# Layer norm moments moved from VectorE to GpSimd in a fused state-space and mixture-of-experts kernel

## The reference, cut to what matters

```python
def _layernorm(x, axis=-1, eps=1e-05):
    m = jnp.mean(x, axis=axis, keepdims=True)
    v = jnp.var(x, axis=axis, keepdims=True)
    return (x - m) / jnp.sqrt(v + eps)

# attn: y = causal convolution of (x B^T) with a Cayley-eigenvalue kernel, times C^T, + D * x
# ffn: 8 experts, h = silu(x Wg) * (x Wu), out = sum over experts of (h Wd) * cw, cw from two softmaxes
x = L0_attn_u
x = x + _layernorm(_L0_attn_ref(_layernorm(x), ...))
x = x + _layernorm(_L0_ffn_ref(_layernorm(x), ...))
```

## Time and profile before

| | us |
|---|---|
| median of 3 runs | 1160.89 (1160.76 to 1161.62) |
| the profiled execution | 1161.8 |
| its span in the trace | 1160.0 |
| PE busy | 1135.0 (98%) |
| DVE busy | 922.2 (80%) |
| ACT busy | 698.0 (60%) |
| POOL busy | 639.0 (55%) |

### The profile page before, as it was taken

The page is one execution under the profiler, slowest core; times in us unless marked ns, Lnnn a source line. Parts: engine busy times, 40 slices in busy tenths (PEclk is TensorE's granted clock), DMA queues, the critical chain, the costliest instruction groups (busy, mean ns, idle before and its releaser), DMA issues.

```text
span 1160.0 us, 16822 instructions
## 1 busy us (share of the span) xinstructions
PE 1135.0 (98%) x5110; PEld 933.6 (80%) x5110; DVE 922.2 (80%) x1999; ACT 698.0 (60%) x1358; POOL 639.0 (55%) x492
## 2 busy tenths in 40 slices
PE   7799999999999999999999999999999999999996
PEld 5577888888888888888888888888888888888885
DVE  7788887888778788887888778788887888778665
ACT  3576565655656556565655656566565665756563
POOL 2686564555646555464645546455464655556453
PEclk8899999999999999999999999999999999999999
DMA  3330212102121020211102021110212102020110
GB/s 96 103 108 19 74 37 55 38 20 77 34 64 47 32 52 28 74 38 56 36 20 83 28 65 46 44 39 28 74 37 65 41 9 81 28 73 28 46 56 10
DMA packets 82697, 57.61 MB, mean 50 GB/s; under 512 B 35344, under 2 KB 64176, under 8 KB 82608
## 3 DMA queue, kind: packets, MB, share of 16 engines
q1 hardware_dynamic: 82608, 56.54, 16.5%
HBM read 48.13 MB, written 8.39 MB: 49 GB/s over the span
## 4 chain that ended last, share of the span: by engine, by line
PE 94%; DVE 3%; issue 1%; POOL 1%; ACT 0%; DMA 0%; SPq 0%; POOLq 0%; ACTq 0%; DVEq 0%
PE g L270 10%; PE u L270 10%; PE y L270 10%; PE g L272 10%; PE g L271 10%; PE y L272 10%; PE u L272 10%; PE u L271 10%; PE y L271 10%; PE n_ps L277 2%; PE m_ps L270 1%; PE m_ps L271 1%; PE m_ps L272 1%; PE m_ps L353 1%; PE m_ps L352 0%
## 5 line engine op out<-in xcount | busy, mean ns | idle before, releaser
L1061 POOL TENSOR_TENSOR hid_lo<-hid,hid_hi 128x512 fp32r<-128x512 f32 x255 | 341.1, 1338 | 409.1 <-ACT hid_hi L541 409.0
L535 ACT ACTIVATE gate<-g 128x512 f32<-128x512 f32 x512 | 305.7, 597 | 326.5 <-PE g L272 324.9
L797 DVE TENSOR_TENSOR hid<-gate,u 128x512 f32<-128x512 f32 x512 | 348.8, 684 | 164.1 <-ACT gate L535 132.7
L541 ACT ACTIVATE hid_hi<-hid 128x512 fp32r<-128x512 f32 x512 | 320.9, 627 | 37.7 <-DVE hid L797 37.1
L803 DVE TENSOR_TENSOR hid_lo<-hid,hid_hi 128x512 fp32r<-128x512 f32 x257 | 211.4, 823 | 1.8
L270 PE MATMUL g<-xe_hi,w_hi 128*128 128x512 f32 x512 | 206.7, 404 | 1.0 <-ACT gate L535 0.9
L270 PE MATMUL u<-xe_hi,w_hi 128*128 128x512 f32 x512 | 200.3, 391 | 4.1 <-DVE hid L797 4.1
L270 PE MATMUL y<-hid_hi,w_hi 128*128 128x512 f32 x512 | 200.4, 391 | 0.4 <-ACT hid_hi L541 0.2
L272 PE MATMUL y<-hid_hi,w_lo 128*128 128x512 f32 x512 | 200.1, 391 | 0.0
L271 PE MATMUL g<-xe_lo,w_hi 128*128 128x512 f32 x512 | 199.9, 390 | 0.0
L272 PE MATMUL g<-xe_hi,w_lo 128*128 128x512 f32 x512 | 199.9, 390 | 0.0
(11 more groups left out here) (173 smaller groups left out, 1141.3 us busy)
## 6 DMA issues: line engine op xcount, KB each, us to landing
cw_b<-cw_scratch SPq DMA_DIRECT2D x128, 256.0 KB, 3.4
x_sb<-x_in SPq DMA_DIRECT2D x16, 256.0 KB, 3.0
x_out<-o_sb SPq DMA_DIRECT2D x16, 256.0 KB, 2.2
out_scratch<-acc_t SPq DMA_DIRECT2D x60, 64.0 KB, 2.2
ffn<-out_scratch SPq DMA_DIRECT2D x15, 256.0 KB, 2.6
stage<-wgate_in SPq DMA_DIRECT2D x8, 256.0 KB, 2.7
stage<-wup_in SPq DMA_DIRECT2D x8, 256.0 KB, 3.0
stage<-wdown_in SPq DMA_DIRECT2D x8, 256.0 KB, 3.9
```

What stands on the lines that cost most here:

```text
L535: nc.scalar.activation(gate[:, k % 2, :], g_ps[k % 2][:], ACT.Silu).then_inc(gate_ready, 1)
L541: nc.scalar.activation(hid_hi[:, k % RING, :], hid[:, k % RING, :], ACT.Copy).then_inc(hi_ready, 1)
L797: nc.vector.tensor_tensor(hid[:, k % RING, :], gate[:, k % 2, :], u_ps[k % 2][:], ALU.mult).then_inc(hid_ready, 1)
L1061: nc.gpsimd.tensor_tensor(hid_lo[:, k % RING, :], hid[:, k % RING, :], hid_hi[:, k % RING, :].bitcast(f32), ALU.subtract).then_inc(lo_pool, 1)
```

## The change

POOL takes the five operations of mean and variance, and the shift, for the norms of x, y and x1 of chunks 1 to 15, and for the output norm of chunks 0 to 14. The two fused operations of DVE that it replaces become plain ones, so mean and variance take six operations on POOL (`moments`): an addition and a subtraction, two multiplications, a multiply-add by constants, and an addition. There are four semaphore steps of its own between them. The mean is kept with its sign turned (`minus_mean`), so that the shift is one multiplication and the norm of x adds it.

DVE keeps `bn_stats`, and the four tiles of the norm of x, which it now does after unit 4 and not unit 3. PE transposes them after unit 6 and not unit 5. The first chunk's mixer and the last chunk's output norm stay as they were, with functions of their own. The diff, cut to its core:

```diff
-TENSOR_AT = {"turn_cw": 4, "turn_x": 5, "bu": 9, "c": 15, "turn_y": 16, "turn_xe": 26,
+TENSOR_AT = {"turn_cw": 4, "turn_x": 6, "bu": 9, "c": 15, "turn_y": 16, "turn_xe": 26,
              "logits": 27}
-VECTOR_AT = {"weights": 1, "stats_x": 1, "var_x": 2, "norm_x": 3, "lo_x": 7, "enter": 8, "scan": 9,
-             "fin_turn": 6, "fin_stats": 14, "fin_var": 14, "fin_shift": 15, "leave": 12, "lo_w": 13, "y": 15, "stats_y": 16, "var_y": 16,
-             "shift": 18, "stats_x1": 22, "var_x1": 22, "shift_x1": 23, "lo_xe": 26, "softmax": 27, "exps": 30,
+VECTOR_AT = {"weights": 1, "stats_x": 1, "norm_x": 4, "lo_x": 7, "enter": 8, "scan": 9,
+             "fin_turn": 6, "fin_stats": 14, "leave": 12, "lo_w": 13, "y": 15, "stats_y": 16,
+             "stats_x1": 22, "lo_xe": 26, "softmax": 27, "exps": 30,
              "products": 31}
-GPSIMD_AT = {"rstd_x": 2, "fin_rstd": 15, "fin_add": 21, "rstd_y": 16, "residual": 18, "rstd_x1": 22}
+GPSIMD_AT = {"norm_x": 2, "fin_norm": 15, "fin_add": 21, "norm_y": 16, "residual": 18, "norm_x1": 22}
...
+            def moments(st, m, ve, link, at):
+                nc.gpsimd.tensor_tensor(m[:], st[:, :, 1:3], st[:, :, 4:6], ALU.add)
+                nc.gpsimd.tensor_tensor(ve[:], st[:, :, 1], st[:, :, 4], ALU.subtract).then_inc(link, 1)
+                pool.wait_ge(link, at + 1)
+                nc.gpsimd.tensor_tensor(m[:], m[:], minus_mean[:], ALU.mult)
+                nc.gpsimd.tensor_tensor(ve[:], ve[:], ve[:], ALU.mult).then_inc(link, 1)
+                pool.wait_ge(link, at + 2)
+                nc.gpsimd.tensor_scalar(ve[:], ve[:], 0.25, LN_EPS, ALU.mult, ALU.add).then_inc(link, 1)
+                pool.wait_ge(link, at + 3)
+                nc.gpsimd.tensor_tensor(ve[:], ve[:], m[:, :, 1], ALU.add).then_inc(link, 1)
+                pool.wait_ge(link, at + 4)
+
+            def mix_norm(c, n):
+                pool.wait_ge(stat_ready, 3 * (c - 1) + n)
+                moments(stats, mv, var_eps, norm_link, 12 * (c - 1) + 4 * (n - 1))
+                nc.gpsimd.tensor_tensor(rstd[:], var_eps[:], half[:], ALU.pow).then_inc(rstd_ready, 1)
+                if n > 1:
+                    pool.wait_ge(rstd_ready, 3 * c + n)
+                    nc.gpsimd.tensor_tensor(shift[:], mv[:, :, 0], rstd[:],
+                                            ALU.mult).then_inc(shift_ready if n == 2 else x1_shift_ready, 1)
...
+            def fin_norms(c):
+                pool.wait_ge(fin_stat, c + 1)
+                moments(stats2, mv2, var_eps2, fin_norm, 4 * c)
+                nc.gpsimd.tensor_tensor(rstd2[:], var_eps2[:], half[:], ALU.pow).then_inc(fin_rstd, 1)
+                pool.wait_ge(fin_rstd, c + 1)
+                nc.gpsimd.tensor_tensor(shift2[:], mv2[:, :, 0], rstd2[:], ALU.mult).then_inc(fin_shift, 1)
```

More of the change, by code:

```diff
@@ L138, in build @@
         cw_t = sb("cw_t", [E * NT, P])
+        minus_mean = sb("minus_mean", [P, NT, 2])
         stats2, mv2 = sb("stats2", [P, NT, 6]), sb("mv2", [P, NT, 2])
@@ L645, in normalise @@
                     last = nc.vector.tensor_scalar(dst[:, j, :], src(j), mv[:, j, 0:1], rstd[:, j:j + 1],
-                                                   ALU.subtract, ALU.mult)
+                                                   ALU.add, ALU.mult)
                 return last
@@ L654, in mix_stats_x, with early_var, scan_link @@
                 dve.wait_ge(x_loaded, 16 * (c + 1))
[L655 to L659, removed]
+                measure(lambda j: x_sb[:, j, :], stats, mix_link if c == 0 else stat_ready)
+            def early_var(n):
+                mean_var(stats, mv, var_eps, mix_link, (0, 5, 8)[n - 1]).then_inc(var_ready, 1)
+            def scan_link(c, n):
+                return 3 + n if c == 0 else 11 + 2 * (c - 1) + n
             def early_shift_x():
@@ L695, in mix_stats_y, with early_shift_y @@
                 dve.wait_ge(y_turned, c + 1)
-                measure(lambda j: n_ps[:, j * P:(j + 1) * P], stats, mix_link)
-            def mix_shift(c):
-                dve.wait_ge(rstd_ready, 3 * c + 2)
+                measure(lambda j: n_ps[:, j * P:(j + 1) * P], stats, stat_ready)
+            def early_shift_y():
+                dve.wait_ge(rstd_ready, 2)
                 shifts(shift, mv, rstd).then_inc(shift_ready, 1)
@@ L703, in mix_stats_x1, with early_shift_x1 @@
                 dve.wait_ge(x1_ready, c + 1)
-                measure(lambda j: x1[:, c % X1S, j, :], stats, mix_link)
-            def mix_shift_x1(c):
-                dve.wait_ge(rstd_ready, 3 * c + 3)
+                measure(lambda j: x1[:, c % X1S, j, :], stats, stat_ready)
+            def early_shift_x1():
+                dve.wait_ge(rstd_ready, 3)
                 shifts(shift, mv, rstd).then_inc(x1_shift_ready, 1)
@@ L779, in fin_stats_last, with fin_mean_var_last, fin_shifts_last @@
                 measure(lambda j: n_ps[:, j * P:(j + 1) * P], stats2, fin_link)
[L781 to L785, removed]
+            def fin_mean_var_last():
+                mean_var(stats2, mv2, var_eps2, fin_link, 0).then_inc(fin_var, 1)
+            def fin_shifts_last():
+                dve.wait_ge(fin_rstd, NCHUNK)
                 shifts(shift2, mv2, rstd2).then_inc(fin_shift, 1)
@@ L827, in _ @@
             nc.vector.memset(pair_mean[:, :, 1], 1.0 / D)
+            nc.vector.memset(minus_mean[:, :, 0], -0.5)
+            nc.vector.memset(minus_mean[:, :, 1], 1.0 / D)
             nc.vector.memset(sharp[:, :, 0, :], 1.0)
@@ L914, in _ @@
             nc.vector.bn_stats(stats[:, 3, :], u_ps[1][:, P:2 * P]).then_inc(mix_link, 1)
-            mix_var(0, 2)
-            mix_shift(0)
+            early_var(2)
+            early_shift_y()
             for j in range(NT + 1):
@@ L932, in _ @@
             last.then_inc(mix_link, 1)
-            mix_var(0, 3)
-            mix_shift_x1(0)
+            early_var(3)
+            early_shift_x1()
             for j in range(NT // 2):
@@ L1021, in _ @@
             fin_stats_last(NCHUNK - 1)
-            fin_mean_var(NCHUNK - 1)
-            fin_shifts(NCHUNK - 1)
+            fin_mean_var_last()
+            fin_shifts_last()
             for j in range(NT):
@@ L1073, in _ @@
                                     pattern=[[-1, P]], channel_multiplier=1).then_inc(const_ready, 2)
-            mix_rstd(0, 1)
+            early_rstd(1)
             pool.wait_ge(trig_ready, 1)
@@ L1081, in _ @@
                                     ALU.subtract).then_inc(proj_split, 1)
-            mix_rstd(0, 2)
-            mix_rstd(0, 3)
+            early_rstd(2)
+            early_rstd(3)
             pool.wait_ge(xn_ready, 2)
@@ L1101, in body @@
                     if not last:
[L1102 to L1105, removed]
+                        if k == GPSIMD_AT["norm_x"]:
+                            mix_norm(c + 1, 1)
+                        if k == GPSIMD_AT["norm_y"]:
+                            mix_norm(c + 1, 2)
                         if k == GPSIMD_AT["residual"]:
                             mix_residual(c + 1, 1 - par)
-                        if k == GPSIMD_AT["rstd_x1"]:
-                            mix_rstd(c + 1, 3)
+                        if k == GPSIMD_AT["norm_x1"]:
+                            mix_norm(c + 1, 3)
                     if not first:
-                        if k == GPSIMD_AT["fin_rstd"]:
-                            fin_rsqrt(c - 1)
+                        if k == GPSIMD_AT["fin_norm"]:
+                            fin_norms(c - 1)
                         if k == GPSIMD_AT["fin_add"]:
@@ L1117, in _ @@
             add_part(NCHUNK - 1, (NCHUNK - 1) % 2, E - 2)
-            fin_rsqrt(NCHUNK - 1)
+            fin_rsqrt_last()
 def sine_rows():
```

32 lines of the change are left out of this document (9 added, 23 removed).

## The result

The changed kernel takes 1180.9 us (median of 4 runs, 1179.85 to 1181.27), the kernel before 1161.26 beside it. The ratio is 1.0168, with a 95% interval from 1.0150 to 1.0185: slower, by some 19.6 us (1.7%). The profiled execution of the changed kernel has 1179.85 us, with a span of 1178.0, against 1161.8 and 1160.0 before.

What follows compares the result with a forecast made beforehand. PE, busy without a gap in the later chunks, was taken to bound the kernel. 15 chunks x (0.60 for x + 0.45 for x1) = 15.8 us on 1160.9 gave 1176.7, say 1177; range 1160.5 to 1203.

Steps and rivals of the forecast that it cites:

- PE has no gap in the later chunks: In the 14 later chunks PE is busy for all 969.40 us, so time DVE gets back is worth nothing there.
- Stall at the transposes of x: After unit 4 DVE's tiles lie beside two POOL operations and reach PE late: 0.6 us a chunk.
- A small operation on POOL takes 0.16 us: In POOL's norm chains, read off a line through 512 and 256 columns; bounds 0.10 and 0.40 us.
- X: Time from POOL being free to the shift of a norm: 2.48 us plus 0.5 for the port, 3.0 us.
- Y's shift comes earlier: At the norm of y, the shift is there at 501.0, so ACT gets 0.35 us earlier on and nothing stalls.
- Stall at the transposes of x1: POOL's chain starts after `hid_lo` of unit 21, so the shift comes 0.27 to 0.62 late, say 0.45 us a chunk.
- Chunk 0: nothing: In chunk 0 the small DVE operations free some tenths and the chain on POOL takes them back: nothing.
- What would show it: In 14 chunks PE idle 14 to 16 us, two waits for `xn` 14 or 15 times each, 70.3 us a chunk.
- the signs against: Small POOL operation over 0.25 us, PE waits for POOL's `hid_lo`, four tiles in 1.1 us, or a 69.2 us chunk.
- only one is late: Rival: only the norm of x late, 1170, or only the shift of x1, 1168; chance 0.20.
- Neither is late: Rival: tiles of x and shift of x1 both in time, 1161, or 1158 if chunk 0's idle goes; 0.15, faster 0.05.
- POOL is much slower with small operations: Rival: the ratio of 1.9 at 512 columns holds for small operations too, 1200, or 1223 at 0.40; chance 0.20.

Runs made afterwards that it cites:

- d: The changed kernel with the norm of x back in its old place and the output's residual sum moved from after unit 21 to after unit 24: 1163.53 us.
- e: The kernel before, all moments on VectorE, with only the norm of x one unit later: 1169.71 us against 1160.66.
- a: The changed kernel with the norm of x back in its old place (tiles after unit 3, transposes after unit 5), moments still on POOL: 1171.05 us.
- b: The changed kernel with DVE's four tiles of the norm of x ahead of the weighing of the last expert, not behind it: 1177.44 us.
- f: The kernel before with only the norm of x1 (moments and shift, chunks 1 to 15) moved to POOL: 1173.78 us against 1160.66.
- c: The changed kernel with POOL's residual sum of the output moved from after unit 21 to after unit 24, behind the norm of x1: 1172.48 us.
- h: The changed kernel with one more small operation and semaphore step in POOL's chain for x1, between power and shift: 1185.34 us.
- g: Kernel d with chunk 1's moments and shifts, which fall into chunk 0's loop, back on DVE: 1161.20 us against 1160.66 for the kernel before.

## Why the prediction was right, step by step

The forecast was 1177 us; measured were 1180.9. In the 14 later chunks the mechanism was the one forecast: both stalls, and no other. In the first chunk it was not, and two errors there offset each other in part.

- *PE has no gap in the later chunks, so DVE's time is worth nothing.* Right. DVE is busy for 59 us less, and d, with no stall left, has 69.20 us a chunk against 69.24. The gain of all that freed time is 0.04 us a chunk, 0.6 in all. The idle time of chunk 0 was not removed either.
- *Stall at the transposes of x, 0.60 us a chunk, from the port.* Right in size and cause. The shift of the place alone costs 0.61 us a chunk (e, 69.86 against 69.24), taking it back gives 0.71 (a). The tiles take the 2.5 us that were worked out, and the second does come just behind POOL's sum, by 0.04 us where 0.05 was said. b shows that the order decides: with no sum between them, the tiles take 2.11 us.
- *A small operation on POOL takes 0.16 us, X is 3.0 us.* The operation takes 0.20 us, the step 0.08 as read, the power 1.02. X is 3.16 us for x1, for y 3.02 (505.94 to 508.96, below), 3.15 in f. The line through two large sizes was 0.04 us short, which over the chain for x1 makes 0.23; the port, at 0.5, costs 0.45 there (the first operation's 0.65 less 0.20) and 0.32 for y (an operation of 0.52).
- *Y's shift comes earlier and hands 0.35 us on.* It does, a little less: it is at 508.96, and ACT waits 1.15 us for it instead of 1.42, so 0.27 us. The timeline of chunk 6 of the changed kernel:

```profile
504.64 1.30 POOL L1087 TENSOR_TENSOR acc<-acc,y_part 128x512 f32<-128x512 f32 x1
508.76 0.20 POOL L1054 TENSOR_TENSOR shift<-mv,rstd 128x4 f32<-128x4 f32 x1
509.00 1.51 ACT L491 ACTIVATE z_sb<-n_ps,shift,rstd 128x128 f32<-128x128 f32 x4 [1.15 <-POOL shift L1054]
```

  Kernel f shows what this is worth: without it, the loss at x1 is 0.80 us a chunk.
- *Stall at the transposes of x1, 0.45 us a chunk (0.27 to 0.62).* Measured 0.54 by c (70.45 less 69.91) and 0.50 as what a keeps over the kernel before; within the bounds. From the lower bound of 0.27, which has all 0.35 handed on, it is 0.08 that y gives back less and 0.16 by which the chain for x1 is longer: 0.51. That the delay of POOL's `hid_lo` of unit 23 is covered by the same stall holds here, but only just: with 0.28 us more (h), 0.15 of it shows ahead of another product.
- *Chunk 0: nothing, besides one of the 15 pairs of stalls.* This is the step that failed. That the small DVE operations free some tenths and the chain on POOL, busy there for 52 of 73 us, takes them back, had no working behind it: no row was read for what stands behind the chain on POOL in chunk 0, and PE awaits its `hid_lo` from there. The pair of stalls, 1.05 us in the sum, isn't there: PE has no wait for `xn` in chunk 0 of the changed kernel, and in e the later place of x adds nothing to it. In their place POOL's chains hold up its own `hid_lo`, and PE waits for that: chunk 0 is 2.25 us longer, and g, with chunk 1's moments on DVE, takes this back. That the sum had 1.05 us there for a cause that doesn't act is luck.
- *The whole sum.* The loss is 19.6 us and not 15.8, 3.8 more. The later chunks give 1.20 us and not 1.05, 0.15 x 14 = 2.1. Chunk 0 gives 2.25 and not 1.05, 1.2 more. The last 0.5 us is left open; the profiled executions differ by up to 1.6 us in the stretch up to unit 3 of chunk 0, in both directions.
- *What would show it.* The two waits came 14 times each, a chunk of 70.45 us and tiles of 2.5 us as said. PE's shown idle time is 11.8 us and not 14 to 16, as the idle time shown is smaller than the loss. A chunk has 4.0 us less of DVE and 5.4 more of POOL. Of the signs against, two came in part: a small operation of 0.65 us, but only beside a `hid_lo` of DVE, and waits of PE for POOL's `hid_lo`, but only in chunk 0.

The rival "only one is late" can be laid beside kernels c and a, where an edit takes one stall out: x alone at 1172.5 against the 1170 worked out, x1 alone at 1171 against 1168, each with chunk 0's loss besides. "Neither is late" needed an X of at most 2.87 us, and X was 3.02 for y and 3.16 for x1; kernel d gets there by moving two steps. "POOL is much slower with small operations" fell: the ratio of 1.9 at 512 columns is 1.3 at 4 (0.20 against 0.15 us). The Trainium skill's advice in "GPSIMD Engine Reference", section "Engine selection", to keep elementwise work on VectorE, gave the right sign here. The ratio of about 2 that it names is not what cost: the operations that moved take 0.20 us and not 0.15, and in d, with all of them on POOL, a later chunk takes no longer than before (69.20 against 69.24 us). It was their place in POOL's queue that cost.

## What to carry to other kernels

- Where the bounding engine has no gap, ask of each moved step not whether the new engine has time on average, but what stands in its queue when the result is wanted. In the changed kernel POOL is idle for 38% of the time, and 0.28 us more on it at the wrong place, once a chunk, cost 4 to 5 us.
- Two changes of place in a hand-written order can cost as much as the work that was moved with them; each should be timed alone. Here the order of two neighbours decided which operation was held up, and the conflict that b moved out of one fell on the next.
- A stretch whose engine load differs from the rest (here the first chunk) needs a working of its own; "nothing" is not one.

## What the runs showed of the hardware that was not expected

- POOL's tensor_tensor takes 0.20 us for 4 and for 8 columns, 0.72 for 256, 1.29 for 512. A semaphore step of POOL to itself takes 0.08 us, as one from DVE to POOL does. The same sizes take 0.15 to 0.17 us on DVE with nothing beside them, so small operations on POOL cost little more than on DVE.
- A small operation on POOL beside a `hid_lo` of DVE, which has two inputs in SBUF, takes 0.65 instead of 0.20 us; in the chains looked at one operation in each is held up so, for 0.52 us (y), 0.65 (x1) or 0.72 (x1 in c).
